# A Swin block on one core: two runs of fc2 rows placed in the attention loop, with the linear stages and SP's transfers in another order

## The reference, cut to what matters

```python
shortcut = x
y = _ln(x, norm1_g, norm1_b)
y = jnp.roll(y, (-SS, -SS), axis=(1, 2))
yw = y.reshape(B, nWh, WS, nWw, WS, C).transpose(0, 1, 3, 2, 4, 5).reshape(B * nW, N, C)
qkv = yw @ qkv_w.T + qkv_b
...
attn = jnp.einsum('bhqd,bhkd->bhqk', q * scale, k)
attn = attn + bias.transpose(2, 0, 1)[None]
attn = attn.reshape(B, nW, HEADS, N, N) + jnp.asarray(_MASK)[None, :, None]
attn = jax.nn.softmax(attn.reshape(B * nW, HEADS, N, N), axis=-1)
o = jnp.einsum('bhqk,bhkd->bhqd', attn, v)
o = o.transpose(0, 2, 1, 3).reshape(B * nW, N, C)
o = o @ proj_w.T + proj_b
...
x = shortcut + o
h = _ln(x, norm2_g, norm2_b)
h = jax.nn.gelu(h @ fc1_w.T + fc1_b, approximate=False)
h = h @ fc2_w.T + fc2_b
return x + h
```

## Time and profile before

| | us |
|---|---|
| median of 3 runs | 4173.28 (4170.92 to 4176.32) |
| the profiled execution | 4170.26 |
| its span, first to last instruction | 4168.4 |
| busy: PE 94%, PEld 74%, DVE 71%, ACT 65%, POOL 51% | 3908.2, 3103.5, 2956.7, 2709.6, 2114.7 |
| TensorE clock granted | 0.995 of full over the span |
| DMA, mean busy share of 16 engines | 34% for the kernel's own transfers |

### The profile page before, as it was taken

One profiled execution on the slowest core, in us unless ns is written; L12 is line 12 of the kernel. 1 busy time (PEld: TensorE's weight loads), 2 busy tenths in 40 slices (PEclk: granted clock), 3 DMA queues, 4 the chain that ended last, 5 costly groups with the idle time before them and its releaser, 6 DMA issues.

```text
span 4168.4 us, 170731 instructions
## 1 busy us (share of the span) xinstructions
PE 3908.2 (94%) x72080; PEld 3103.5 (74%) x72080; DVE 2956.7 (71%) x8221; ACT 2709.6 (65%) x4608; POOL 2114.7 (51%) x3476
## 2 busy tenths in 40 slices
PE   3899999999999999999999999999999999999998
PEld 2677777777777777777777777777777777777776
DVE  6777777677777767777777777677777777777773
ACT  1666666666666666666666666666666666666664
POOL 4455555555555545545455555455555555555553
PEclk8999999999999999999999999999999999999999
DMA  2333333333333333333333333333333333333332
GB/s 80 104 110 107 107 107 112 104 109 110 107 108 109 111 104 108 107 108 106 106 107 108 107 107 114 100 110 109 108 107 109 109 107 108 108 107 108 111 110 59
DMA packets 609583, 441.61 MB, mean 106 GB/s; under 512 B 142083, under 2 KB 608371, under 8 KB 608819
## 3 DMA queue, kind: packets, MB, share of 16 engines
q1 hardware_dynamic: 608355, 428.88, 33.9%
q0 software_dynamic: 464, 1.81, 0.1%
HBM read 106.14 MB, written 51.46 MB: 38 GB/s over the span
## 4 chain that ended last, share of the span: by engine, by line
PE 62%; DVE 19%; DMA 7%; issue 6%; ACT 4%; SPq 2%; DVEq 0%; POOL 0%; ACTq 0%; POOLq 0%
PE ps L774 11%; PE ps L788 10%; PE ps L804 9%; PE ps L721 9%; DMA sums<-pv_sb 7%; PE ps L758 6%; PE ps L753 6%; PE ps L877 4%; DVE x L663 3%; DVE k_lo L617 3%; DVE neg_max L571 3%; PE ps L886 3%; DVE yT_lo L602 3%; DVE v_own L669 2%; ACT k_hi L466 2%
## 5 line engine op out<-in xcount | busy, mean ns | idle before, releaser
L571 DVE TENSOR_REDUCE neg_max<-ps 113x8 f32<-113x392 f32 x2048 | 1052.5, 555 | 245.8 <-PE ps L721 244.3
L408 ACT ACTIVATE probs<-ps 113x784 f32<-113x784 f32 x1024 | 829.0, 823 | 380.9 <-PE ps L758 377.7
L804 PE MATMUL ps<-w,hid 128*112 128x128 f32 x7168 | 862.4, 275 | 7.9 <-issue 7.2
L804 PEld LDWEIGHTS ps<-w,hid 128*112 128x112 f32 x7168 | 816.6, 177 | 33.4 <-issue 11.0
L758 PE MATMUL ps<-st_q,st_k 128*49 128x196 f16 x8192 | 696.7, 249 | 0.0
L753 PE MATMUL ps<-bias,eye_k 106*64 106x392 f16 x4096 | 686.1, 332 | 1.2 <-ACT probs L408 0.7
L425 ACT ACTIVATE hid<-ps,col 128x448 f32<-128x448 f32 (+1 forms) x1024 | 511.3, 576 | 234.8 <-PE ps L788 234.8
L721 PE MATMUL ps<-mx_k,mx_q 128*49 128x196 f16 x8192 | 561.8, 252 | 76.1 <-DVE neg_max L571 48.9
L378 POOL TENSOR_TENSOR x_b<-x,fc_b 112x896 f32<-112x896 f32 x128 | 267.7, 2092 | 607.9 <-DVE y_out L563 607.9
L774 PE MATMUL ps<-probs,v_own 113*32 113x49 f32 x32768 | 489.6, 209 | 54.7 <-issue 53.0
L758 PEld LDWEIGHTS ps<-st_q,st_k 128*49 128x49 f16 x8192 | 444.1, 105 | 124.5 <-issue 1.6
(11 more groups left out here) (109 smaller groups left out, 6948.5 us busy)
## 6 DMA issues: line engine op xcount, KB each, us to landing
st_k<-k_hi SPq DMA_DIRECT2D x256, 196.0 KB
st_q<-q_hi SPq DMA_DIRECT2D x1024, 49.0 KB
oT_raw<-pv_sb SPq DMA_DIRECT2D x256, 196.0 KB, 2.7
x_in<-in_x SPq DMA_DIRECT2D x224, 196.0 KB
x_res<-in_x SPq DMA_DIRECT2D x224, 196.0 KB
out_y<-y_out SPq DMA_DIRECT2D x224, 196.0 KB
mx_q<-q_hi SPq DMA_DIRECT2D x128, 196.0 KB
mx_k<-k_hi SPq DMA_DIRECT2D x512, 49.0 KB
```

What stands on the lines that cost most here:

```text
L408: nc.scalar.activation(probs[0:KP, w % 4, :].rearrange("p (b c) -> p b c", b=2), ps[0:KP, b:b + 2, 0:HB * WT], ACT.Exp).then_inc(s_exp, 1)
L571: nc.vector.tensor_reduce(neg_max[0:KP, :, 2 * b:2 * b + 2, w].rearrange("p e g -> p g e"), ps[0:KP, b, :].rearrange("p (g c) -> p g c", g ...
L804: last = mm(tokens_of(6)[0:TP, i, :], hid[:, c, i * TP:(i + 1) * TP], w_2[:, c, :], start=(c == 0), stop=(c == CH - 1))
```

## The change

It changes the order of PE's, ACT's, DVE's and SP's lists, some banks, and some shapes. The arithmetic stays, but for `yT_hi`, which ACT now writes straight from PSUM, and `yT_lo`, which DVE now takes as PSUM minus `yT_hi`.

- **fc2** is cut in rows 0-2 and rows 3-6 (`FC2_PARTS`), both in bank 7. Rows 3-6 of band t-2 come first, in the loop of step t: two rows after the logits of window 1, two after those of window 5. Rows 0-2 follow in step t+1, after the transposes. `finish` of rows 3-6 is last in DVE's step.
- **The loop** goes by single windows: logits w (both banks), `pv` of the pair before when w is 2, 4 or 6, the two fc2 rows when w is 1 or 5, coarse logits w. The wait for the maxima stays one for each bank. All `pv` go to bank 6, each after ACT has copied the one before.
- **Linear stages** on PE: last `pv`, transposes of `z2`, of `z1`, of the maxima, fc2 rows 0-2, fc1 chunks 0 and 1, k, q (now banks 6 and 7), fc1 chunks 2 and 3, spread, v, output projection. fc1 has four chunks of 784 tokens (two matmuls of 392) in place of eight blocks of 448 or 336; gelu, `h_hi`, `h_lo`, `k_hi` and `q_hi` are one instruction of 784 each. v waits for `q_lo`.
- **SP**: `x_in` ahead of `oT_raw`; two of the four `neg_maxT` transfers behind `r_rows`; `mx_k` ahead of `mx_q`, and as soon as `k_hi` is there; `y_out` ahead of the fifteen of `st`.

The core of the diff:

```diff
+                if exists(n) and n != 0:
+
+                    sp.wait_ge(s_t1, n)
+                    band_dmas(sp, xr, x_in, n, edge(n), False, s_x)
+                n = t - 1
+                if exists(n):
                     if past(n, 0):
                         sp.wait_ge(s_oT, n)
                     for im in range(2):
                         sp.dma_start(oT_raw[:, im, :], pv_sb[im:C:4, :, :]).then_inc(s_o_dma, 16)
-                n = t + 2
-                if exists(n) and n != 0:
-
-                    sp.wait_ge(s_t1, n)
...
+                n = t
+                if exists(n):
+                    neg(n, (2, 3), odd(0))
...
                     else:
                         sp.wait_ge(s_init, 2)
...
+                    sp.wait_ge(s_hi, 2 * n + 2)
+                    sp.dma_start(mx_q[edge(n)][0:C:4, :, :],
+                                 q_hi[:, :, :, :].rearrange("c w m q -> c (w m q)")).then_inc(s_mx_dma, 16)
```

```diff
+            def gelu(n, c):
+                if c == 0 and past(n, 0):
+                    act.wait_ge(s_fc2, 2 * n)
+                act.wait_ge(s_fc1, CH * n + c + 1)
+                bank = 2 + 2 * (c % 2)
+                nc.scalar.activation(hid[:, c, :].rearrange("p (b q) -> p b q", b=2), ps[:, bank:bank + 2, 0:HT],
                                      ACT.Gelu, bias=col[:, BF + c:BF + c + 1], scale=1 / W_SCALE).then_inc(s_gelu, 1)
...
+                n = t - 2
+                if exists(n):
+                    act.wait_ge(s_t2, n + 1)
+                    if past(n, 0):
+                        act.wait_ge(s_fc1, CH * n)
+                    nc.scalar.activation(h_hi[:, :].rearrange("p (i c) -> p i c", c=TP),
+                                         tokens_of(2)[:, 0:WS, 0:TP], ACT.Copy).then_inc(s_h_hi, 1)
                 n = t + 1
...
+                    dst = yT_hi[odd(1)][:, :, :, 0:WT].rearrange("p w m (i j) -> p w m i j", i=WS)
...
+                if exists(t - 2):
+                    load_table(ACT.Gelu)
+                    gelu(t - 2, 0)
+                    gelu(t - 2, 1)
                 n = t + 1
...
+                    gelu(t - 2, 2)
+                    gelu(t - 2, 3)
...
-                        if w % 2 and w > 1:
+                        if w % 2 == 0 and w > 0:
                             copy_pv(t, w // 2 - 1)
```

```diff
+                    pe.wait_ge(s_vown_b, 2 * n + 2)
                 else:
-                    pe.wait_ge(s_pv_sb, NU * n + u - 1)
+                    pe.wait_ge(s_pv_sb, NU * n + u)
...
-                        last = mm(ps[32 * r:32 * r + VC, 6 + u % 2, first:first + WT],
+                        last = mm(ps[32 * r:32 * r + VC, 6, first:first + WT],
```

The wait ahead of `pv` (u over 0) is thus for the copy of the `pv` just before. fc1, fc2 and the body of PE:

```diff
+            def fc1(n, c):
+                if c == 0:
+                    pe.wait_ge(s_h_lo, n + 1)
+                elif c == 1 and exists(n + 1):
+                    pe.wait_ge(s_exp, NW * (n + 2))
+                elif c > 1:
+                    pe.wait_ge(s_gelu, CH * n + c - 1)
+                bank = 2 + 2 * (c % 2)
                 for k, (ww, hh) in enumerate(((w1_hi, h_hi), (w1_hi, h_lo), (w1_lo, h_hi))):
-                    last = mm(ps[:, 2 + m % 4, 0:(i1 - i0) * TP], ww[:, c * C:(c + 1) * C], hh[:, i0 * TP:i1 * TP],
-                              start=(k == 0), stop=(k == 2))
+                    for b in range(2):
+                        last = mm(ps[:, bank + b, 0:HT], ww[:, c * C:(c + 1) * C], hh[:, b * HT:(b + 1) * HT],
+                                  start=(k == 0), stop=(k == 2))
                 last.then_inc(s_fc1, 1)
 
...
+            def fc2(n, p, i):
+                first, end = FC2_PARTS[p]
+                if i == first and p == 1:
+                    pe.wait_ge(s_gelu, CH * (n + 1))
+                    if exists(n + 2):
+                        pe.wait_ge(s_vown, 2 * (n + 2) + 1)
+                        pe.wait_ge(s_vown_b, 2 * (n + 2) + 1)
+                    elif n > 0:
+                        pe.wait_ge(s_fin, 2 * n)
+                if i == first and p == 0:
+                    pe.wait_ge(s_fin, 2 * n + 1)
+                for c in range(CH):
+                    last = mm(ps[0:TP, 7, (i - first) * C:(i - first + 1) * C], hid[:, c, i * TP:(i + 1) * TP], w_2[:, c, :],
+                              start=(c == 0), stop=(c == CH - 1))
+                if i == end - 1:
+                    last.then_inc(s_fc2, 1)
```

```diff
                 if exists(t - 3):
-                    fc2(t - 3, 2, 4)
+                    for i in range(*FC2_PARTS[0]):
+                        fc2(t - 3, 0, i)
+                if exists(t - 2):
+                    fc1(t - 2, 0)
+                    fc1(t - 2, 1)
                 n = t + 1
                 if exists(n):
-                    pe.wait_ge(s_y_hi, n + 1)
+                    pe.wait_ge(s_y_lo, n + 1)
...
+                    for w_hi, w_lo, bank in ((wk_hi, wk_lo, 0), (wq_hi, wq_lo, 6)):
+                        if bank == 6 and exists(t):
+                            pe.wait_ge(s_negT, t + 1)
+                        if bank == 6 and exists(t - 3):
+                            pe.wait_ge(s_fin, 2 * (t - 3) + 2)
+                        for k, (ww, yy) in enumerate(((w_hi, high), (w_hi, low), (w_lo, high))):
+                            for im in range(2):
+                                last = mm(ps[:, bank + im, 0:BT], ww[:, :], yy[im], start=(k == 0), stop=(k == 2))
+                        last.then_inc(s_qk, 1)
...
+                    fc1(t - 2, 2)
+                    fc1(t - 2, 3)
...
-                        pe.wait_ge(s_lo, 4 * (t + 1) + 2)
+                        pe.wait_ge(s_lo, 2 * (t + 1) + 1)
...
-                    pe.wait_ge(s_negT, n + 1)
+                    if exists(t + 1):
+                        pe.wait_ge(s_lo, 2 * (t + 2))
```

```diff
-                for u in range(NU):
+                for w in range(NW):
                     if exists(t):
-                        logits(t, 2 * u, edge, odd(0), (0, 1))
-                        logits(t, 2 * u + 1, edge, odd(0), (0,))
+                        logits(t, w, edge, odd(0))
+                        if w % 2 == 0 and w > 0:
+                            pv(t, w // 2 - 1)
+                    if exists(t - 2) and w in (1, 5):
+                        for i in (0, 1):
+                            fc2(t - 2, 1, FC2_PARTS[1][0] + w // 2 + i)
                     if exists(t + 1):
-                        max_logits(t + 1, 2 * u, edge)
-                    if exists(t):
-                        logits(t, 2 * u + 1, edge, odd(0), (1,))
-                        if u > 0:
-                            pv(t, u - 1)
-                    if exists(t + 1):
-                        max_logits(t + 1, 2 * u + 1, edge)
+                        max_logits(t + 1, w, edge)
```

286 lines of the change are left out of this document (119 added, 167 removed).

## The result

| | us |
|---|---|
| before, median of 6 runs on the same chip | 4172.1 (4163.6 to 4176.32) |
| after, median of 6 runs | 4142.73 (4133.69 to 4149.97) |
| ratio, 95% interval | 0.993 (0.9915 to 0.9944) |
| profiled execution of after, its span | 4133.69, 4131.9 |
| clock granted to TensorE | 0.995 |

The change makes the kernel 0.7% faster, 29 us where 41 were forecast; the time was to be 4132. Of the six runs of after three stand at 4133.7 to 4136.3 and three at 4149.2 to 4150.0. The profile is of one of the lower three.

The account below looks back on a forecast made before the run. PE's list was taken as the bound, with 2.35 of 31.67 us a step in waits. Work of 29.3 plus remaining and new waits gave 31.15, with 0.2 added 31.35: 41 us less, 4132 us; range 4052 to 4226.

Parts of the forecast that it names:

- (a): Coarse logits at the first windows wait for DVE's maxima; 0.85 us a step, forecast to go.
- (b): Pauses in `pv` where PE's next 256 instructions have not arrived; 0.65 us a step, 0.6 forecast to go.
- (c): Linear stages: PE waits for `q_lo`, `yT_hi` and `yT_lo`; 0.85 us a step, forecast to go.
- (d): Last `pv` waits for the exponential of window 7; a new wait of 0.8 us a step.
- (e): Coarse logits of window 3: the second bank's maxima come late, a new wait of 0.3 us a step.
- (f): v waits for `q_lo`, behind `x_in` and DVE's statistics; 0.35 us late, bounds 0 to 1.3.
- (g): Spread waits for `r_rows`, 0.25 us; with (f) a maximum, 0.5 us a step for both.
- the addition: 0.2 us a step added because (f) to (h) are near misses of several chains.
- (h): First coarse logits wait for `mx_q`, now issued last after `r_rows`; 0.2 us, bounds 0 and 1.0.
- PE's work: PE's step without waits: as many matmuls and columns as before, so unchanged at 29.3 us.
- Rival 2: Pauses in `pv` are a property of `pv` itself and stay: 77 us over forecast, 4210 us; chance 0.12.
- Rival 3: Transfers on SP's single list come late; each 0.1 us is 13 us, 4234 us at 0.8 over; chance 0.14.

Follow-up runs that it names:

- The kernel with single fc2 rows: The changed kernel with the loop's four fc2 rows one by one behind the logits of windows 1, 3, 5 and 7: 4085.47 us, ratio 0.9797.
- the kernels from 3.51 us on: All kernels of the rate table except before and before with `pv` apart: 256 instructions take 3.51 us or more without pauses; pauses 0.01 to 0.16 us a step.

## Why the prediction was right and where it was not

The mechanism and the sum of one step held (31.37 measured, 31.35 forecast), and the ratio was off by 0.3%. By its terms, with the measured mean of a step:

| term | forecast | measured | read from |
|---|---|---|---|
| (a) first maxima | gone | gone | coarse block at window 1: 0.364 |
| (b) pauses, rest | 0.05 | 0.04 and 0.13 | four `pv`, start to start, in the two profiles |
| (c) linear stages | gone | gone | `q_lo` is no releaser at fc1 any more |
| (d) exponential of window 7 | 0.8 | 0.69 | block of window 7, 1.146 - 0.458 |
| (e) window 3 | 0.3 | 0.30 | its block, 0.638 - 0.343 |
| (f), (g) v and spread, with the addition | 0.7 | 0.33 | end of fc1 to the output projection |
| (h) `mx_q` | 0.2 | 0.19, of it some 0.15 for `x1` | first coarse block's start |
| PE's work | 29.3 | 29.8 | the rest |

- **"PE's work is the same"** is the step that failed. As many matmuls, but set among others: two groups of float32 fc2 rows now stand between float16 blocks, at 0.3 us each for what surrounds them, and the `z2` transposes follow `pv` directly (0.72, 2014.50 to 2015.22). The prediction costed fc2 rows only by the groups of before, where less surrounds them: the x16 behind `pv` takes 1.84, 0.09 over its rows (2005.69 to 2007.53), the x16 ahead of k 1.75 in the steps in which k does not wait, the x24 ahead of the spread 2.72 where it takes 2.62 now. So 0.6 - 0.09 - 0.10 = 0.41 come from fc2. The transposes add 0.05 (0.67 before) and fc1, now the block ahead of the spread, 0.09 (2.08 in the median step, 1.99 ahead of k). Together that is 0.55 for the 0.5. The kernel with single fc2 rows priced the largest part.
- **(f) and (g)** were too dear by 0.37, which by chance hid the first error. (f) is the one that exists: 24.7 us at v for `q_lo` and 13.0 at the spread for `k_lo`, both behind the statistics of `x_in`. (g) all but does not: the spread waits 1.6 us in all for `r_rows`. The reciprocal was early, since `sums` came in time (4.9 us of waits for 116.5).
- **(d)** was 0.1 too dear: the coarse block ahead of a `pv` takes 0.46 and not the 0.34 that the prediction set against the wait. **(h)** has the right size by luck in part: in most steps the first coarse block starts 0.15 us after DVE's `x1` ends, `mx_q` or not, and `mx_q` comes late in one step of four.
- **(b)** came out right in size with one of its two reasons wrong. Two close `pv` are not what the pauses hang on; the rate of the loop, which the prediction worked out as 2.9 and 4.0 us for 256 instructions, orders the kernels down to the last 0.15 us, and the places of the pauses bear out its packets of 256. Rival 2, pauses as a property of `pv` itself, falls with the `pv` row of after, 0.911 us for 1.06, and with the pauses outside `pv`. The sentence of the Trainium skill on which it leaned (Runtime: NRT & Kernel Launch, Instruction fetch mechanics: the cost of crossing a block's bound is "mostly hidden") fits the kernel after, where 0.04 to 0.13 of 31.4 us are left, and not the kernel before, with 0.66.
- **The time.** 0.30 us a step less is 38 us, and the profiled execution is 36.6 below that of before, 4133.69 for 4170.26. The median is 29 below, since half of its runs stand some 15 us higher; the profile of a run at that height has 13 us more of pauses and `mx_q` waits. That the times of an unchanged program lie up to 28 us apart (4128 to 4156) was no part of the forecast.
- **Rival 3** (late transfers) has its mechanism and not its case: `x_in` behind `oT_raw` costs 131 us. DVE waits 1.5 us a step for `x_in` even now (194.5 / 128), more than the mark of 1 us at which the prediction called itself wrong. That mark was set badly: of these 1.5 us no more than 0.33 reach PE, at v and the spread.

The row of the kernel before on which the 1.84 rests:

```profile
2005.69 2.00 PE L804 MATMUL ps<-w,hid 128*112 128x128 f32 x16
```

Still open: why the packets come later in one run of the same program than in another, and why the kernels from 3.51 us on differ in what is left. No run here moves the bounds of the packets and nothing else.
